# Whole-bank windows for the score maxima, and 32-column tiles for the small matmuls

## The reference

```python
qh = einsum('bnd,hde->bhne', layernorm(x), Wq)      # 16 heads, 8 wide
kh = einsum('bmd,hde->bhme', ctx, Wk)               # 1601 keys
vh = einsum('bmd,hde->bhme', ctx, Wv)
att = softmax(einsum('bhne,bhme->bhnm', qh, kh) * 0.125, axis=-1)
out = einsum('bhnm,bhme->bhne', att, vh)            # heads side by side
x = x + tanh(g_xattn) * (concat(out) @ Wo.T)
```

```python
probs = softmax(layernorm(x) @ router_w.T); top2 = top_k(probs, 2), normalised
x = x + tanh(g_ffn) * sum_e cw[:, e] * (gelu(xn @ w1[e].T + b1[e]) @ w2[e].T + b2[e])
```

## Time and profile before

| | |
|---|---|
| timed runs, median of 3 | 1344.58 us (1342.93 to 1349.27) |
| profiled execution, span from first to last instruction | 1360.3 us, mean granted TensorE clock 0.975 |
| instructions | 38009 |
| TensorE matmuls (PE) | 1289.7 us busy, 95% |
| TensorE weight loads (PEld) | 627.0 us, 46% |
| VectorE (DVE) | 1157.6 us, 85%; 985.2 us of it the 1024 window reductions of L1546 |
| ScalarE (ACT) | 1094.7 us, 80%; 892.2 us of it the 1664 exponentials of L1077 |
| GpSimd (POOL) | 546.7 us, 40% |

### The profile page before, as it was taken

The page is one execution under the profiler, slowest core; times in us unless marked ns, Lnnn a source line. Parts: engine busy times, 40 slices in busy tenths (PEclk is TensorE's granted clock), DMA queues, the critical chain, the costliest instruction groups (busy, mean ns, idle before and its releaser), DMA issues.

```text
span 1360.3 us, 38009 instructions
## 1 busy us (share of the span) xinstructions
PE 1289.7 (95%) x14041; PEld 627.0 (46%) x14041; DVE 1157.6 (85%) x2268; ACT 1094.7 (80%) x2190; POOL 546.7 (40%) x1208
## 2 busy tenths in 40 slices
PE   4899999999999999999999999999999999998992
PEld 2243444444444444444444444444444433497882
DVE  7897999999999999999999999999999999355334
ACT  1487898988889888898989898888989888864561
POOL 3231426262626262535353444444453512145441
PEclk7698999999999999999999999999999999999997
DMA  3232121212121212121222222222211110386886
GB/s 91 76 86 82 45 67 51 70 47 75 46 78 42 83 35 66 52 64 54 64 59 60 63 58 66 58 64 58 67 52 39 49 40 6 98 258 196 252 262 231
DMA packets 61077, 112.67 MB, mean 83 GB/s; under 512 B 13052, under 2 KB 36476, under 8 KB 60748
## 3 DMA queue, kind: packets, MB, share of 16 engines
q1 hardware_dynamic: 54043, 97.67, 24.6%
q0 software_dynamic: 4320, 8.99, 2.0%
q10 hardware_dynamic: 2529, 3.58, 0.8%
HBM read 52.77 MB, written 13.71 MB: 49 GB/s over the span
## 4 chain that ended last, share of the span: by engine, by line
PE 75%; DVE 16%; SPq 3%; issue 3%; DMA 1%; ACT 1%; POOL 0%; POOLq 0%; ACTq 0%; DVEq 0%
PE pv L821 27%; PE st L772 14%; PE mxp L794 13%; DVE mx L1546 13%; PE st L1038 5%; PE mxp L1048 4%; PE st L879 4%; PE st L888 2%; SPq L401 2%; PE st L900 1%; PE st L851 1%; PE st L923 1%; PE st L863 1%; PE st L933 1%; DVE x_sb L1741 1%
## 5 line engine op out<-in xcount | busy, mean ns | idle before, releaser
L1546 DVE TENSOR_REDUCE mx<-mxp 128x2 f32<-128x804 f32 x1024 | 985.2, 987 | 71.1 <-PE mxp L794 60.8
L1077 ACT ACTIVATE arena<-st 128x512 f32<-128x512 f32 (+1 forms) x1664 | 892.2, 595 | 88.8 <-PE st L772 82.2
L821 PE MATMUL pv<-arena 128*32 128x256 f32 x6656 | 535.6, 394 | 0.5 <-ACT pv_sb L1084 0.4
L794 PE MATMUL mxp<-kpack,qpack 48*128 48x402 bf16 x2048 | 457.0, 344 | 16.2 <-DVE mx L1546 14.8
L772 PE MATMUL st<-qpack,kpack 51*128 51x256 bf16 (+1 forms) x3328 | 449.2, 273 | 2.4 <-DMA qpack<-mxT 2.1
L772 PEld LDWEIGHTS st<-qpack,kpack 51*128 51x128 bf16 (+1 forms) x3328 | 199.4, 97 | 202.4 <-ACT arena L1077 108.0
L794 PEld LDWEIGHTS mxp<-kpack,qpack 48*128 48x128 bf16 x2048 | 142.6, 93 | 167.0 <-DVE mx L1546 94.3
L821 PEld LDWEIGHTS pv<-arena 128*32 128x32 f32 x6656 | 131.6, 108 | 177.0 <-issue 89.3
L659 POOL CAST mxs<-nmx 128x8 bf16<-128x8 f32 x64 | 12.4, 193 | 263.3 <-DVE nmx L1554 263.2
L1218 ACT ACTIVATE arena<-st,bias 128x256 f32<-128x256 f32 (+1 forms) x172 | 74.1, 438 | 54.7 <-PE st L1038 38.4
L702 POOL DMA_INDIRECT results<-ysb,idx x71 | 68.9, 971 | 89.2 <-DVE ysb L1683 58.2
(11 more groups left out here) (194 smaller groups left out, 908.7 us busy)
## 6 DMA issues: line engine op xcount, KB each, us to landing
kpack<-ksp SPq DMA_DIRECT2D x750, 50.0 KB
arena<-in_w12T SPq DMA_DIRECT2D x43, 576.0 KB
arena<-in_ctxT SPq DMA_DIRECT2D x15, 800.5 KB, 4.5
qpack<-qsp SPq DMA_DIRECT2D x187, 32.0 KB
xblk<-rows SPq DMA_DIRECT2D x28, 132.0 KB
rows<-in_pads SPq DMA_DIRECT2D x8, 264.0 KB
arena<-results SPq DMA_DIRECT2D x8, 256.0 KB, 6.9
arena<-results ACTq DMA_DIRECT2D x8, 256.0 KB, 7.2
```

What stands on the lines that cost most here:

```text
L794: eng.matmul(mxp[pair % MX_BUFS][:, rg, 0:WIN], qpack[rows, b % 2, g * JJ + jj, t * P:(t + 1) * P], kpack[rows, b % 2, g * JJ + jj, WSTART ...
L821: ins = eng.matmul(pv[32 * j:32 * j + 32, 0:N], vaug[0:n, b % 2, kt, at:at + 32], pt[0:n, (2 * u + rg) % PT_BUFS, jj * N:(jj + 1) * N], st ...
L1077: eng.activation(pt[0:n, c % PT_BUFS, :], ring[bank_of["S", u, p]][0:n, :], ACT.Exp, scale=SCALE).then_inc(s_exp, 1)
L1546: eng.tensor_reduce(mx[:, tj, w, :], mxp[windows_done % MX_BUFS][:, :, 0:WIN], AX.X, ALU.max).then_inc(s_red, 1)
```

## The change

Three things change, and the program's other parts stay.

**Windows.** A window is a whole bank, 512 columns, so three cover 1536 keys. The 65 keys left over, for both query tiles and both head pairs of a group, go side by side into one more bank pair (4 x 65 = 260 columns an array half, in eight matmuls), reduced by one instruction with a four-level pattern. A group needs 13 window slots in place of 16, a batch 52 in place of 64. TensorE's columns per array half and group are 12 x 512 + 260 = 6404 in place of 16 x 402 = 6432.

**Strips.** `keys`, `values`, `queries`, `project`, `route` and `rank_tokens` issue each matmul as four, on 32 columns of the weights each, at tile positions (0, 0), (0, 32), (0, 64) and (0, 96), all four with the same moving operand. The output's place in the bank is the same.

**The order.** The constants that place side work and windows are new: key chunk 3 in unit 8 for 6, value chunk 3 in unit 30 for 28, turned heads in 3 and 47 for 2 and 42, the third turn of the maxima in 31 for 34, rows and queries in 36 and 42 for 39 and 43, their norm in 23 for 26; 17 windows ahead of unit 0 in place of 24, and the lead at a batch's start is 22 slots in place of 30.

```diff
--- before.py
+++ after.py
@@ -30,12 +30,13 @@
 GROUPS = B * NG
 KT = -(-M // P)
 UNITS = NG * KT
-WIN = 402
-WSTART = [0, 400, 800, M - WIN]
-NW = len(WSTART)
+WIN = 512
+NF = M // WIN
+REST = M - NF * WIN
+NW = NF + 1
 RG = 2
 JJ = HG // RG
-NMX = JJ * NT * NW
+NMX = JJ * NT * NF + 1
 MP = 1604
 KCH = [(0, 401), (401, 400), (801, 400), (1201, 400)]
 NK = len(KCH)
@@ -87,28 +88,29 @@
 GUESS = float(0x5F3759DF)
 NEWTON = 3
 N_W2 = 4
+STRIP = 32
 MIX = (NBK - LARGE) // 3
 ORDER = list(range(LARGE - 2 * MIX))
 for k in range(MIX):
     at, small_at = LARGE - 2 * MIX + 2 * k, LARGE + 3 * k
     ORDER += [at, small_at, small_at + 1, at + 1, small_at + 2]
 PHASES = [(0, FULL, SL), (FULL, LARGE - FULL, SL), (LARGE, NBK - LARGE, SS)]
-K_AT = {1: 0, 4: 1, 5: 2, 6: 3}
-V_AT = {25: 0, 26: 1, 27: 2, 28: 3}
-HEADS_AT = {2: 0, 42: 1}
-TURN_AT, PLACE_AT = {8: 1, 22: 2, 34: 3, 47: 4}, {9: 1, 23: 2, 35: 3, 48: 4}
+K_AT = {1: 0, 4: 1, 5: 2, 8: 3}
+V_AT = {25: 0, 26: 1, 27: 2, 30: 3}
+HEADS_AT = {3: 0, 47: 1}
+TURN_AT, PLACE_AT = {8: 1, 22: 2, 31: 3, 47: 4}, {9: 1, 23: 2, 31: 3, 49: 4}
 POST_AT = {7: "C", 9: "F", 21: "L", 23: "R"}
-X_AT, Q_AT = 39, 43
-FIRST_K_AT = {7: 0, 9: 1, 10: 2, 11: 3}
+X_AT, Q_AT = 36, 42
+FIRST_K_AT = {6: 0, 9: 1, 10: 2, 11: 3}
 RANK_AT, LAST_RANK_AT, COUNT_AT, PLAN_AT = 46, 35, 38, 40
-L_NORM_AT, X_NORM_AT = 10, 26
-LOGITS_AT, EXP_AT, ROUTE_AT = 24, 26, 27
+L_NORM_AT, X_NORM_AT = 10, 23
+LOGITS_AT, EXP_AT, ROUTE_AT = 24, 26, 26
 ROWS_AT, LAST_ROWS_AT = {1: 40, 2: 42, 3: 44}, {9: 0, 10: 1, 11: 2, 12: 3}
-FIRST, LEAD = 24, 30
-WINDOWS_AT = ("1011011110111111111111101001101110011111110111100111",
-              "1101111020000000000001101211100011100000011000120000")
-FIRST_WINDOWS_AT = ("1000000000000000000000000000000000000000000000000000",
-                    "1121121212221112111121121222111211211212111211121110")
+FIRST, LEAD = 17, 22
+WINDOWS_AT = ("0111111121010111101011111110111110110111101111111101",
+              "0000100001000000010001000010000010010000100000000001")
+FIRST_WINDOWS_AT = ("0000110001001000000000000000101100000000010100100100",
+                    "1211110102111011111111112110101111112011101110011011")
 PER_BATCH = NG * NMX
 ISSUED, FIRST_ISSUED = [[sum(int(at[q][r]) for r in range(UNITS) for q in range(2) if 2 * r + q < c)
                          for c in range(2 * UNITS)] for at in (WINDOWS_AT, FIRST_WINDOWS_AT)]
@@ -753,6 +755,15 @@
 
         @block.tensor
         def _(eng):
+            def strips(dst, weights, moving, **flags):
+
+                m = weights.shape[1]
+                for c in range(0, m, STRIP):
+                    n = min(STRIP, m - c)
+                    ins = eng.matmul(dst[c:c + n, :], weights[:, c:c + n], moving,
+                                     tile_position=(0, c), **flags)
+                return ins
+
             freed = [(s_k3, c + 1) for c in range(ST_BUFS)] + [(s_pvs, COPIES)]
 
             def scores(u, rg, beside):
@@ -782,8 +793,6 @@
             def window(G, m, rg):
 
                 b, g = divmod(G, NG)
-                tj, w = divmod(m, NW)
-                t, jj = divmod(tj, JJ)
                 pair = G * NMX + m
                 if m == 0:
                     eng.wait_ge(s_qd[b % 2], 16 * PACKS * (b // 2 + 1))
@@ -791,10 +800,21 @@
                 if pair >= MX_BUFS:
                     eng.wait_ge(s_red, pair - MX_BUFS + 1)
                 rows = slice(rg * RSTEP, rg * RSTEP + MAXROW)
-                eng.matmul(mxp[pair % MX_BUFS][:, rg, 0:WIN],
-                           qpack[rows, b % 2, g * JJ + jj, t * P:(t + 1) * P],
-                           kpack[rows, b % 2, g * JJ + jj, WSTART[w]:WSTART[w] + WIN],
-                           start=True, stop=True).then_inc(s_mxp, 1)
+                if m < NMX - 1:
+                    tj, w = divmod(m, NF)
+                    t, jj = divmod(tj, JJ)
+                    ins = eng.matmul(mxp[pair % MX_BUFS][:, rg, 0:WIN],
+                                     qpack[rows, b % 2, g * JJ + jj, t * P:(t + 1) * P],
+                                     kpack[rows, b % 2, g * JJ + jj, w * WIN:(w + 1) * WIN],
+                                     start=True, stop=True)
+                else:
+                    for tj in range(NT * JJ):
+                        t, jj = divmod(tj, JJ)
+                        ins = eng.matmul(mxp[pair % MX_BUFS][:, rg, tj * REST:(tj + 1) * REST],
+                                         qpack[rows, b % 2, g * JJ + jj, t * P:(t + 1) * P],
+                                         kpack[rows, b % 2, g * JJ + jj, NF * WIN:M],
+                                         start=True, stop=True)
+                ins.then_inc(s_mxp, 1)
 
             def maximum(G, m):
                 for rg in range(RG):
@@ -860,8 +880,7 @@
                     freed[i] = s_qhi, b + 1
                     dst = ring[i]
                 eng.wait_ge(s_xnT, b + 1)
-                eng.matmul(dst[:, 0:N], wq_sb[:, :], xnT[:, :], start=True, stop=True
-                           ).then_inc(s_qp, 1)
+                strips(dst[:, 0:N], wq_sb[:, :], xnT[:, :], start=True, stop=True).then_inc(s_qp, 1)
 
             def keys(b, c):
                 k0, kn = KCH[c]
@@ -876,8 +895,8 @@
                     eng.wait_ge(s_ctx[b % 2], 16 * (b // 2 + 1))
                 if b == 0 and k0 == HALF:
                     eng.wait_ge(s_ctx_b, 16)
-                eng.matmul(dst[:, 0:kn], wk_sb[:, :], ctx_sb[:, b % 2, k0:k0 + kn],
-                           start=True, stop=True).then_inc(s_kp, 1)
+                strips(dst[:, 0:kn], wk_sb[:, :], ctx_sb[:, b % 2, k0:k0 + kn],
+                       start=True, stop=True).then_inc(s_kp, 1)
 
             def values(b, c):
                 i = bank_of["V", b, c]
@@ -885,9 +904,9 @@
                 eng.wait_ge(*freed[i])
                 for t in range(tn):
                     n = key_rows(t0 + t)
-                    ins = eng.matmul(ring[i][0:n, t * D:(t + 1) * D],
-                                     ctx_sb[:, b % 2, (t0 + t) * P:(t0 + t) * P + n],
-                                     wv_sb[:, :], start=True, stop=True)
+                    ins = strips(ring[i][0:n, t * D:(t + 1) * D],
+                                 ctx_sb[:, b % 2, (t0 + t) * P:(t0 + t) * P + n],
+                                 wv_sb[:, :], start=True, stop=True)
                     if t == tn - 1:
                         ins.then_inc(s_vp, 1)
                 freed[i] = s_v, NV * b + c + 1
@@ -920,8 +939,8 @@
                 if b == 0:
                     eng.wait_ge(s_w2, 16 * N_W2)
                 for t in range(NT):
-                    ins = eng.matmul(ring[i][:, t * P:(t + 1) * P], concT[:, t * P:(t + 1) * P],
-                                     wo_sb[:, :], start=True, stop=True)
+                    ins = strips(ring[i][:, t * P:(t + 1) * P], concT[:, t * P:(t + 1) * P],
+                                 wo_sb[:, :], start=True, stop=True)
                 ins.then_inc(s_f3p, 1)
                 freed[i] = s_res, b + 1
 
@@ -930,8 +949,8 @@
                 eng.wait_ge(*freed[i])
                 eng.wait_ge(s_x2T, b + 1)
                 for t in range(NT):
-                    ins = eng.matmul(ring[i][:, t * NE:(t + 1) * NE], xn2T[:, t * P:(t + 1) * P],
-                                     rw_sb[:, :], start=True, stop=True)
+                    ins = strips(ring[i][:, t * NE:(t + 1) * NE], xn2T[:, t * P:(t + 1) * P],
+                                 rw_sb[:, :], start=True, stop=True)
                 ins.then_inc(s_rp, 1)
                 freed[i] = s_lgt, b + 1
 
@@ -943,9 +962,9 @@
                     eng.wait_ge(s_tri, 2)
                 eng.wait_ge(s_base, b + 1)
                 dst = ring[i][:, 0:NT * NE]
-                eng.matmul(dst, tri_bf[:, :], mask[:, :, :].rearrange("p t e -> p (t e)"), start=True, stop=False)
-                eng.matmul(dst, ones_bf[:, :], before[:, :, :].rearrange("p t e -> p (t e)"), start=False,
-                           stop=True).then_inc(s_rk, 1)
+                strips(dst, tri_bf[:, :], mask[:, :, :].rearrange("p t e -> p (t e)"), start=True, stop=False)
+                strips(dst, ones_bf[:, :], before[:, :, :].rearrange("p t e -> p (t e)"), start=False,
+                       stop=True).then_inc(s_rk, 1)
                 freed[i] = s_rkc, b + 1
 
             def count_tokens(phase):
@@ -1539,12 +1558,17 @@
 
             def maximum(G, m):
                 nonlocal windows_done
-                tj, w = divmod(m, NW)
                 eng.wait_ge(s_mxp, RG * (windows_done + 1))
                 if m == 0 and G > 0:
                     eng.wait_ge(s_nmx, NT * G)
-                eng.tensor_reduce(mx[:, tj, w, :], mxp[windows_done % MX_BUFS][:, :, 0:WIN],
-                                  AX.X, ALU.max).then_inc(s_red, 1)
+                src = mxp[windows_done % MX_BUFS]
+                if m < NMX - 1:
+                    tj, w = divmod(m, NF)
```

(5 more changed lines are left out.)

## The result

The changed kernel took 1310.74 us in the median of four runs (1307.59 to 1312.38), the kernel before 1345.68 in four (1342.93 to 1349.27): a ratio of 0.9745, 95% interval 0.972 to 0.977. The forecast was 1313. The profile of the changed kernel is of the fastest of its four executions, 1307.59 us.

What follows compares the result with a forecast made beforehand. TensorE's own time was taken to bound the attention stage. A steady batch's -1.9 us gave -27 over batches 1 to 14; with batch 0, batch 15, prologue and expert stage, -31 on 1344.6 made 1313 us, range 1298 to 1336.

Steps and rivals of the forecast that it cites:

- TensorE's own time bounds the stage: Attention stage: of a 70.63 us batch only 1.7 us is TensorE waiting; VectorE is 4 us behind it.
- The strips, -2.4: Side steps in a batch: fewer changes of array shape and shorter weight loads save 2.4 us, bounds 1.2 and 2.9.
- Windows on TensorE, +0.2: Scores with windows in a batch: columns hardly change, no extra weight loads counted, +0.2 us.
- Windows on VectorE, -1.0: Window reductions in a batch: 57.2 us against 58.2, so VectorE saves 1.0 us and stays near 65.5.
- I take the waits as 1.7 before and 2.0 after.: TensorE's waiting in a batch: grows from 1.7 to 2.0 us, bounds 1 and 4, chiefly in units 28 to 49.
- The prologue, -0.5: Before the first scores: bound by the first group's maxima, fewer windows ahead fall into their placement's wait, -0.5 us.
- Batch 0, -3: First batch: -2 us from keys, values and queries, -1 for the even chance of the slow clock stretch's 5 us.
- Batch 15, -1: Last batch: it has projection, logits and ranks of batch 14, -1 us.
- The expert stage, +0.5: Expert stage: batch 15's strips change the array shape amid whole-array work, 3 x 0.2, +0.5 us.
- Rival A: Strip steps: records are fed too slowly, +2.4 us a batch, 1380 us, slower than before; chance 8%.
- Rival B: Attention batches: VectorE becomes the bound, period 69.7 us, -0.9 a batch, 1328 us; chance 20%.
- Rival C: Third turn of the maxima: stops of 1 us a batch, or a clock fall behind them, 1330 to 1345; chance 6%.

Runs made afterwards that it cites:

- e0: The kernel before, unchanged, profiled a second time: span 1344.7 us, ratio 1.000 to the kernel before.
- e1: The kernel before with the strips alone, windows of 402 columns and all placements as before: ratio 0.988 to the kernel before.
- e2: The changed kernel with whole-array matmuls in place of the strips, so new windows and new places only: ratio 0.996 to the kernel before.
- e3: The changed kernel with two strips of 64 columns in place of four of 32: ratio 0.991 to the kernel before.
- e8: The changed kernel with the leftover pair's half on rows 0 to 63 issued behind the scores of rows 64 to 127: ratio 0.974 to the kernel before.
- e4: The kernel before with the new places of side work alone, old windows and strings, no strips: ratio 1.015 to the kernel before.
- e7: The changed kernel with one window slot beside the scores of every unit of a steady batch: ratio 0.980 to the kernel before.
- e9: The kernel before with strips and new places of side work, but windows of 402 columns and their old strings: ratio 1.000 to the kernel before.
- e6: The changed kernel with 21 windows ahead of unit 0 in place of 17, four fewer in batch 0: ratio 0.976 to the kernel before.
- e5: The changed kernel with batch 15's projection, logits and ranks on the whole array again: 1322.73 us against 1355.77 for the kernel before on that chip.

## Why the prediction was right

The time was 1310.7 for 1313, -34.9 us for -31. That it is so near is partly luck. By stages, e0's profiled execution against the changed kernel's: the prologue gave -3.0 for the -0.5 forecast, batches 1 to 14 -36.2 for -27, batch 0 +1.6 for -3, batch 15 +0.4 for -1, the expert stage -1.8 for +0.5. That is -38.9 in this pair of executions, and -34.9 in the medians. Term by term, a batch each:

- **TensorE's own time bounds the stage.** This held only in part. In e1 2.5 us less of TensorE's time gave 1.27 of period; with the new windows, strings and places it gave most (2.48 of own time, 2.07 of period, from e2 to the changed kernel). The 1.7 us of waiting before was 2.0.
- **The strips, -2.4.** Own time -2.52 (e1), -2.48 (e2 to after). The shape's part held: the start is 0.11 us later with 64 columns (e3); the weights' part was not measured by itself. Key chunk 1.24 forecast, 1.24 measured; value chunk 1.45, 1.44 at the least; logits 0.73, 0.67; ranks 0.1 saved, 0.11.
- **Windows on TensorE, +0.2.** +0.38. One term was mis-sized by more than that: the leftover pair's block was set at 0.44 and is 0.56, four times 0.12. It was counted by columns, and the order of issue between the array's halves was left out (e8 gives it back). Against it, the forty blocks with one window take 0.54 at the least for the 0.55 assumed.
- **Windows on VectorE, -1.0.** Durations are 1.22 and 0.69, and reductions back to back start every 1.13 us, for 1.14. VectorE's busy time fell by 1.8, from 66.5 to 64.6, where "near 65.5" was forecast.
- **"I take the waits as 1.7 before and 2.0 after."** This is the step that failed, in sign: 2.0 before and 1.5 after. I argued from one reduction being longer than the unit around it. Where the slots stand among the side work counts as well: e4 moves only the side work (+1.55 of waiting), e7 only the slots (+0.42). Before, twelve blocks a batch had two windows and took 0.773 us in the mean for a least 0.668, 1.3 of the 2.0 us; after, four have, at 0.846 for 0.757, 0.4 of the 1.5. Taken by itself, the change of windows and strings is worth 2.5 us a batch with strips (e9 to after) and 2.1 without (e4 to e2), all of it less waiting; how much is the size of the windows and how much their places stays open. The forecast also put the waits into units 28 to 49; over half of them stand in units 8 to 25. The errors, +0.2 for the windows, -0.8 for the waits and -0.1 for the strips, leave -2.63 for -1.9.
- **The prologue, -0.5.** -3.0. The step "the seven windows fewer ahead of unit 0 fall into the wait for their placement" failed: the scores stand behind those windows in TensorE's own queue (e6).
- **Batch 0, -3.** 77.0 us in e0, 82.3 in the profile shown ahead, 78.6 after: a gain against the one and a loss against the other. The wait at unit 39 is in all three (1.64, 2.06 and 2.04 us), so the earlier third turn did not remove it. Behind it the profile shown ahead has 10.2 us at the 1.2 GHz level, the changed kernel 6.8, and e0 none.
- **Batch 15, -1.** +0.4, in one pair of executions; no run looks into it.
- **The expert stage, +0.5.** Not to be told from nothing (e5).

Rival A, strips fed too slowly, is out: a value chunk with its values takes 1.44 us at the least, for the 1.45 forecast, where A had a full value chunk's 64 records take 1.78 by themselves. The Trainium skill ("TensorE: Matmul & The Clock Gate", Part 1, Wait - 56ns, not 53.3ns?) gives about 62 ns per MATMUL with hardware decode off. As a mean this neither showed nor was refuted: the batch has 956 matmul records in 68 us, 71 ns each. But the 16 of the logits start within 0.12 us, and the 32 of a value chunk take 0.98 us (1.44 less 0.46), so the estimate of 2.0 us did not come true; that of 1.0 can't be told from what the columns take. Rival B, VectorE as the bound, is half the truth for e1 and not for the change. Rival C did not show in the steady batches: the third turn fits. But the scores do wait for a placement, that of the third group's maxima in unit 23, which stands behind SyncE's key transfers. The forecast had these keys "with 20 units to spare". It looked at which transfers the moved places pass, and not at GpSimd, whose 17.2 us for the splits stay the same while the units beside them get shorter.

## What to carry to other kernels

Here a step on tiles of another shape than the step before it starts 0.11 us later. Small side steps that have the shape of the work they stand behind save that, and shorter weights save more: 0.20 us in all for a key chunk of 1.45, 0.44 for logits of 1.11. When TensorE and the engine that drains it are within some per cent of each other, split a period into least block times and waiting: half of the time taken off TensorE came back as waiting until the windows were cut and placed anew, and the new places of side work alone made the kernel slower. When a saving doesn't move the period, take the difference unit by unit, and batch by batch: here a mean hid ten batches of one kind and two of another. And look at the engine that no share of the page points to: GpSimd, 40% busy, has a chain of fixed length, and it set when a transfer could start.

## What the hardware showed that I had not expected

Matmuls on the two halves of the array's rows did not start strictly in the order of issue. In the leftover block the scores of rows 64 to 127, issued behind all four small matmuls of the other half, start at 415.46, behind the first and ahead of the second (415.49). Yet they did not start when their half was free (415.36, by the estimate above); they came only once the first of those ahead had started (415.45). e3's last value chunk, with a strip of 64 columns and one of a single column, is the dearest form of all: 1.24 us, where the whole array takes 0.93 and strips of 32 take 0.78.
